# Second attention of a two-layer network: scores of the second half moved in front of both outputs, keys of the second half behind them

## What is computed

```python
x = x + L0_xattn(layernorm(x), ctx)   # 16 heads of 8
x = x + L0_ffn(layernorm(x))          # 8 experts, the best two of each token
x = x + L1_xattn(layernorm(x), ctx)   # 16 heads of 64, low-rank parts, 4 extra context tokens
x = x + L1_ffn(layernorm(x))          # router, 16 experts, each takes 32 tokens of a batch

# L1_xattn, of one batch:
q_in = x @ Wq + lora(x)
k_in, v_in = org_ctx @ Wk + lora, org_ctx @ Wv + lora        # 124 tokens of the context
out = softmax(q k^T / 8) v + softmax(q ipa_k^T / 8) ipa_v    # ipa: the last 4 tokens
return out @ Wo + bo + lora(out)
```

## Time and profile before

| | |
|---|---|
| Times of 3 runs | 515.51, 519.51, 519.55 us, median 519.51 |
| Profiled execution | 518.3 us, of which the span of the instructions is 516.6 |
| PE busy | 494.2 us, 96% of the span |
| PEld busy | 381.7 us, 74% |
| DVE busy | 355.0 us, 69% |
| ACT busy | 291.0 us, 56% |
| POOL busy | 234.5 us, 45% |
| Chain that ended last | PE 85%, DVE 8%, ACT 2%, issue 2% |
| DMA | 14.48 MB, mean 28 GB/s |

### The profile page before, as it was taken

The page is one execution under the profiler, slowest core; times in us unless marked ns, Lnnn a source line. Parts: engine busy times, 40 slices in busy tenths (PEclk is TensorE's granted clock), DMA queues, the critical chain, the costliest instruction groups (busy, mean ns, idle before and its releaser), DMA issues.

```text
span 516.6 us, 13574 instructions
## 1 busy us (share of the span) xinstructions
PE 494.2 (96%) x5113; PEld 381.7 (74%) x5113; DVE 355.0 (69%) x1000; ACT 291.0 (56%) x984; POOL 234.5 (45%) x331
## 2 busy tenths in 40 slices
PE   4799999999999999999999999999999999999996
PEld 3566766656667777877788776788857897799995
DVE  5788989766695687566875756757966688535553
ACT  3366565454576876657776568665674444413332
POOL 5745545035365434665345753333331990090440
PEclk9999999999899999999999999999999999999999
DMA  8910000000001101111000000022202200001001
GB/s 231 198 34 4 3 3 3 3 3 6 4 0 33 34 2 34 34 33 33 3 2 3 3 3 1 1 65 64 63 1 56 70 0 1 1 13 32 1 2 42
DMA packets 21873, 14.48 MB, mean 28 GB/s; under 512 B 5929, under 2 KB 21137, under 8 KB 21809
## 3 DMA queue, kind: packets, MB, share of 16 engines
q1 hardware_dynamic: 20704, 13.31, 9.7%
q10 hardware_dynamic: 1104, 0.30, 0.3%
HBM read 12.30 MB, written 1.05 MB: 26 GB/s over the span
## 4 chain that ended last, share of the span: by engine, by line
PE 85%; DVE 8%; ACT 2%; issue 2%; DMA 1%; ACTq 1%; POOL 1%; DVEq 0%; POOLq 0%
PE bank L1792 9%; PE bank L1551 6%; PE bank L1558 6%; PE bank L1721 6%; PE bank L1538 5%; PE bank L1510 5%; PE bank L1463 5%; PE bank L1530 5%; PE bank L1801 5%; PE bank L1521 5%; PE bank L1374 5%; PE bank L1808 3%; PE bank L1609 3%; PE bank L1359 3%; PE bank L1344 1%
## 5 line engine op out<-in xcount | busy, mean ns | idle before, releaser
L498 POOL TENSOR_TENSOR work<-work,rsum 128x496 f32<-128x496 f32 x64 | 64.1, 1012 | 122.7 <-DVE rsum L789 122.7
L1150 ACT ACTIVATE work<-bank,negmax 128x124 f32<-128x124 f32 x256 | 89.9, 383 | 52.6 <-DVE ipa_s L775 52.5
L533 POOL TENSOR_SCALAR work<-work,slot 128x128 f32<-128x128 f32 x64 | 49.6, 792 | 48.3 <-DVE slot L864 29.4
L1150 ACT ACTIVATION_READ_ACCUMULATOR work<-bank,negmax 128x1 f32 x256 | 58.0, 226 | 0.0
L1792 PE MATMUL bank<-work 128*128 128x256 f32 x224 | 53.4, 382 | 0.0
L1014 DVE SCALAR_TENSOR_TENSOR work<-work,bank 128x256 f32<-128x256 f32 x64 | 26.9, 421 | 33.0 <-ACT work L1302 32.8
L1302 ACT ACTIVATE work<-bank 128x256 f32<-128x256 f32 x64 | 24.5, 383 | 40.6 <-PE bank L1792 29.1
L306 DVE TENSOR_TENSOR x_all<-bank,x_all 128x128 f32<-128x128 f32 x16 | 4.7, 292 | 59.5 <-PE bank L1721 57.1
L481 POOL TENSOR_TENSOR work<-work 128x512 f32<-128x512 f32 (+2 forms) x48 | 39.2, 818 | 12.1 <-DVE work L745 9.6
L1792 PEld LDWEIGHTS bank<-work 128*128 128x128 f32 x224 | 40.4, 191 | 4.6 <-DVE work L1017 0.2
L773 DVE TENSOR_REDUCE negmax<-bank 128x4 f32<-128x496 f32 x64 | 42.5, 664 | 0.0
(11 more groups left out here) (197 smaller groups left out, 1109.7 us busy)
## 6 DMA issues: line engine op xcount, KB each, us to landing
work<-in_L_ffn_w_dram SPq DMA_DIRECT2D x42, 128.0 KB, 2.3
x_all<-in_x_dram SPq DMA_DIRECT2D x4, 256.0 KB, 5.7
out_dram<-x_all SPq DMA_DIRECT2D x4, 256.0 KB, 2.5
ctx_all<-in_ctx_dram SPq DMA_DIRECT2D x4, 192.0 KB, 5.9
ctx_all<-in_L_ffn_w_dram SPq DMA_DIRECT2D x6, 128.0 KB, 2.2
work<-in_L_xattn_Wq_dram SPq DMA_DIRECT2D x1, 512.0 KB, 6.2
work<-in_L_xattn_Wo_dram SPq DMA_DIRECT2D x1, 512.0 KB, 9.0
work<-in_L_ffn_We_dram SPq DMA_DIRECT2D x1, 512.0 KB, 6.5
```

What stands on the lines that cost most here:

```text
L498: pool.tensor_tensor(part, part, rsum1[:, b % 2, CH * n:CH * n + CH].unsqueeze(2).broadcast_to((128, CH, ORG)), ALU.mult).then_inc(Z.norm, 1)
L533: ins = pool.tensor_scalar(ohw_of(e)[:, k, :], count[:, :], slot[:, h, 0, k, e % E1:e % E1 + 1], slot[:, h, 1, k, e % E1:e % E1 + 1], ALU. ...
L1150: ins = act.activation(p1[:, b % 2, n, c, 0:ORG], blocks(bank[n])[:, c, 0:ORG], ACT.Exp, bias=negmax1[:, b % 2, h:h + 1], accum_out=sums1[ ...
```

## The change

It moves calls and changes no computation. On TensorE, `scores(b, 1)` goes from behind ffn 0 to behind ffn 1, directly in front of outputs 0; keys 1 goes behind outputs 1; and ffn 0 goes in front of queries 1, except in the rounds of `head_of`. On ScalarE, `weighted(g)` goes in front of the copy of queries 1 (except in those rounds), the copy of outputs 1 and the extra tokens in front of the copy of keys 1, and powers 2 and 3 behind the copy of inputs. On VectorE, `shifted` 2 and 3 go behind `weighted`, `summed` 1 in front of the copy of turn 2, and `ipa_norm` in front of `summed` 2 and 3. On GpSimd, `experts_sum` goes in front of norms 2 and 3. The core of the diff:

```diff
@@ gpsimd, round1
                     rstds(b + 3, b + 4)
+                if there(b + 4):
+                    experts_sum(b + 4)
                 if there(b):
                     norm(b, 2)
                     norm(b, 3)
-                if there(b + 4):
-                    experts_sum(b + 4)
@@ vector, round1
-                if there(b):
-                    shifted(b, 2)
                 if b == 12:
                     hidden(0)
+                if there(b):
+                    summed(b, 1)
                 if there(t):
                     turned(t, 2)
...
-                if there(b):
-                    shifted(b, 3)
                 if there(f):
                     dve.wait_ge(Z.k0, f + 1)
...
                 if there(g):
                     weighted(g, bank[7])
                 if there(b):
-                    summed(b, 1)
+                    shifted(b, 2)
+                    shifted(b, 3)
                 if b == 15:
                     onehot(3)
                 if there(b):
+                    ipa_norm(b)
                     summed(b, 2)
                     summed(b, 3)
-                    ipa_norm(b)
@@ scalar, round1
                 if there(b):
                     powers(b, 1)
+                if there(g) and not j:
+                    weighted(g, bank[7])
                 if b == 15:
                     turned(t, 1)
                 if there(f):
                     queries(f, 1)
...
-                if there(g):
+                if j:
                     weighted(g, bank[7])
-                if there(b):
-                    powers(b, 2)
...
-                if there(b):
-                    powers(b, 3)
...
-                if there(b):
-                    act.activation(ipa_s[:, b % 2, :, :], ipa_s[:, b % 2, :, :], ACT.Exp).then_inc(Z.ipa_exp, 1)
...
                 if there(t):
                     outputs(t, 0)
+                if b == B:
+                    gathered(6)
+                if there(t):
+                    outputs(t, 1)
+                if there(b):
+                    act.wait_ge(Z.maxed, CH * b + 4)
+                    act.activation(ipa_s[:, b % 2, :, :], ipa_s[:, b % 2, :, :], ACT.Exp).then_inc(Z.ipa_exp, 1)
...
-                if there(t):
-                    outputs(t, 1)
...
                 if there(b + 2):
                     inputs(b + 2)
+                if there(b):
+                    powers(b, 2)
+                    powers(b, 3)
                 if there(f):
                     values(f, 0)
@@ tensor, round1
                 if j:
                     head_logits(j, bank[7])
+                elif there(g):
+                    after(pe, Z.xT, b + 2)
+                    ffn(g, 0, bank[7])
                 if there(f):
                     queries(f, 1, *((Z.p_sb, CH * t + 1) if there(t) else (Z.q_sb, 2 * f)))
...
-                if there(g):
-                    if j:
-                        pe.wait_ge(F.step, HEAD_STEPS * j + 1)
+                if j:
+                    pe.wait_ge(F.step, HEAD_STEPS * j + 1)
                     ffn(g, 0, bank[7])
-                if there(b):
-                    scores(b, 1)
...
                     ffn(g, 1, bank[7])
+                if there(b):
+                    scores(b, 1)
+                if b == 15:
+                    gather(2)
+                    tell(3, G.xg, 2)
                 if there(t):
                     outputs(t, 0, *p_copied(t, 2))
+                if b == B:
+                    gather(6)
+                if there(t):
+                    outputs(t, 1, *p_copied(t, 3))
...
                 if there(f):
                     keys(f, 1, Z.k0_sb, f + 1)
...
-                if there(t):
-                    outputs(t, 1, *p_copied(t, 3))
```

More of the change, by code:

```diff
@@ L1203, in round1 @@
             def round1(b):
-                f, t, g = b + 1, b - 1, b + 4
-                if head_of(b):
-                    head_turned(head_of(b), bank[7])
+                f, t, g, j = b + 1, b - 1, b + 4, head_of(b)
+                if j:
+                    head_turned(j, bank[7])
                 if there(b):
@@ L1222, in round1 @@
                     route_tanh(0)
-                if there(g):
+                if j:
                     weighted(g, bank[7])
-                if there(b):
-                    powers(b, 2)
                 if b == 15:
                     gathered(0)
-                if there(b):
-                    powers(b, 3)
-                if b == 15:
                     turned(t, 3)
@@ L1238, in round1 @@
                     turned(t, 3)
-                if there(b):
-                    act.activation(ipa_s[:, b % 2, :, :], ipa_s[:, b % 2, :, :], ACT.Exp).then_inc(Z.ipa_exp, 1)
-                if head_of(b):
-                    head_powers(head_of(b))
+                if j:
+                    head_powers(j)
                 if there(t):
                     outputs(t, 0)
+                if b == B:
[5 more added lines that the diff above has]
+                    act.activation(ipa_s[:, b % 2, :, :], ipa_s[:, b % 2, :, :], ACT.Exp).then_inc(Z.ipa_exp, 1)
                 if b == 12:
@@ L1250, in round1 @@
                     gathered(2)
-                if b == B:
-                    gathered(6)
                 if b == -1:
@@ L1680, in round1 @@
                     route_turn(1, bank[7])
[L1681 to L1685, removed]
                 if there(f):
```

## The result

The changed kernel takes 543.64 us (median of 6 runs, 542.24 to 546.22) against 519.33 us (6 runs, 515.51 to 519.85). The ratio is 1.0499, with a 95% interval of 1.0461 to 1.0538. It is slower by 24 us, where 15.5 were forecast. The profiled execution of it took 545.58 us, its span is 543.8.

The account below looks back on a forecast made before the run. TensorE, busy for the whole 15.58 us of a steady round, was taken as the bound. Terms of 11.2 + 1.2 - 0.4 - 0.3 + 3.8 = 15.5 on the profiled 518.3 gave 533.8, plus 1.2 made 535.0; range 523 to 545.

Parts of the forecast that it names:

- What bounds the kernel, and the drains: Steady rounds: TensorE always busy; array-shape changes fall from six to three, saving 0.5 a round, 15.08 us on TensorE alone.
- What the second scores covered: Fourth turn: reached at 6.0, but ScalarE's chain to the copy of queries 1 takes 6.99; TensorE stands 1.0, round +0.5.
- Powers 2 and 3 late, xn held: Start of next round: late summed(b, 3) and held xn delay first shifted from 1.20 to 1.92; round 16.82, +1.24.
- the part of the lock: Shared port of VectorE and GpSimd: norm(b, 3) holds xn; a round costs +1.24 with it, +0.86 without.
- The sum: Whole kernel: steady rounds 11.2 and special rounds added to 15.5 us more, giving 535.0.
- The term of the steady rounds: Nine rounds (2 to 4, 6 to 11) at +1.24 each, 11.2 us together.
- alike: Rounds 10 and 11, with more VectorE work on both sides of the change, priced as steady rounds at +1.24 each.
- That stretch: Round 15 to the last projection: +1.8 for round 15 and about +2.0 for the last round, +3.8 together.
- rival (1): TensorE stays the bound and only the drains go: 14 x 0.5 = 7 less, 512.5; chance 0.05.
- Rival (2): TensorE's stand stays near its floor, xn not held, tail covered: 0.5 to 0.86 a round, 522 to 530; chance 0.18.
- Rival (3): Stands of 1.7 in 13 rounds lower the clock in a third to all: +7 to +22, 542 to 557; chance 0.12.
- The range: Time of the changed kernel: 523 to 545 us, likeliest 535, about 0.1 chance below and 0.1 above.

Follow-up runs that it names:

- keys_last: Kernel before, with only keys 1 behind outputs 1 on TensorE and ScalarE's copy of outputs 1 before that of keys 1; 516.18 us, ratio 0.9967.
- mended: Changed kernel: weighted after copy of queries 1, summed 2 and 3 at round's end, second expert half behind outputs, VectorE's weighted behind shifted 3; 514.15 us.
- Experts_first: Kernel before, with only first expert half before queries 1 on TensorE and weighted before the copy of queries 1 on ScalarE; 517.72 us, ratio 0.9996.
- sums_last: Changed kernel, with summed 2 and 3 on VectorE moved from in front of the residual to the end of the round; 525.05 us.
- norm_after_xn: Changed kernel, with GpSimd's norm(b, 3) waiting until VectorE has written xn(b + 3); 536.75 us, ratio 1.0370.
- filled: Changed kernel, with eight unread transposes added on TensorE in front of the fourth turn of rounds 1 to 14; 544.79 us, ratio 1.0511.
- copy_first: Changed kernel, with weighted(g) on ScalarE behind the copy of queries 1 again; 538.82 us, ratio 1.0390.

## Why the prediction was right or wrong, point by point

**What bounds the kernel, and the drains:** right. The block lengths of 0.92 to 0.99 came out, keys_last measured them alone as 0.31 to 0.34 us of the 0.34 worked out, in the rounds without a new wait, and mended has rounds of 15.17 where 15.08 were summed. The Trainium skill's rule that a change of tiling mode drains TensorE (TensorEngine Tiling (Array Packing), Key Properties) holds with these sizes; used alone it would have given the wrong sign for this change.

**What the second scores covered:** right, and shown from both sides. Experts_first has the same ScalarE chain under cover and costs nothing; the changed kernel has it bare and stands 1.39 us. ScalarE's chain took 4.88 us from the first powers to the end of the copy, 4.92 were summed.

**Powers 2 and 3 late, xn held:** right in mechanism, and nearly in size. The first shifted came at 1.80, not 1.92, the turn at 7.69, not 7.74. Sums_last took away the whole of it (0.59 a round), norm_after_xn the part of the lock (0.41). In sums_last the first shifted starts at 1.20 and the copy of queries 1 ends at 6.96, as summed (6.99); the turn comes at 7.10, 0.14 later, as it comes 0.15 behind the copy in the changed kernel, where I had counted 0.03 for the signal.

**The sum:** this is the step that failed. The term of the steady rounds held to 0.01 us. Outside them the profiled span grew by some 10 us more than summed (27.2 without the 1.5 of the first attention, against 15.5). The wrong step is that the special rounds were priced as if VectorE's steps behind summed(b, 3) were those of a steady round: I had counted only onehot(4) as queued there, and had taken rounds 10 and 11 "alike". At the end of round 9 three steps that make masks (`picks`) stand between summed(9, 3) and the residual:

```profile
303.13 0.18 DVE L789 RECIPROCAL rsum<-sums 128x4 f32<-128x4 f32 x1 [1.20 <-ACT work L1149]
303.22 0.34 DVE L804 TENSOR_REDUCE e_mask<-ident 128x16 f32<-128x128 f32 x1
...
304.34 0.28 DVE L306 TENSOR_TENSOR x_all<-bank,x_all 128x128 f32<-128x128 f32 x1
```

These 1.1 us, on top of the late summed, put the first shifted of round 10 at 3.27 of the round instead of 1.65. Its +3.93 are 1.24 as summed, 1.1 for the masks and 1.6 for the clock. In filled and in copy_first, without a drop, round 10 costs 1.1 more than a steady round does; in sums_last, where the masks can run early, 0.2 more. Round 14, forecast +1.1, took +3.3. There the same place holds, at the end of round 13, the probabilities and the first eight of the router. VectorE and TensorE at the start of round 14 of the changed kernel:

```profile
375.64 0.18 DVE L789 RECIPROCAL rsum<-sums 128x4 f32<-128x4 f32 x1 [1.20 <-ACT work L1149]
375.73 0.26 DVE L833 TENSOR_REDUCE ex_sum<-probs 128x1 f32<-128x128 f32 x1
...
378.14 0.29 DVE L306 TENSOR_TENSOR x_all<-bank,x_all 128x128 f32<-128x128 f32 x1
```

```profile
378.49 1.16 PE L1530 MATMUL bank<-xT,work 128*128 128x128 f32 x8 [1.63 <-DVE x_all L306]
```

Before, these 2.4 us of router steps ran while TensorE made the outputs and the projection; now they cannot start before powers(13, 3) are done, and the residual behind them, for which TensorE's queries wait, comes 3 us into the round. At the end of round 14 it is the same with `eight(0, 3)` and `places(0)`. The rule that I had applied to the residual, name what is queued behind the waiting instruction, was not applied round by round. Sums_last, which lets these steps run early, took 2.7 us off round 14, and 5.0 off the stretch behind it. That stretch was forecast +3.8 and took +6.4; 1.2 of the 2.6 between them is the second half of the clock's drop there, as measured above; by my estimate from this price the whole drop cost about 2.4, so here it is the clock, and in rounds 10 and 14 the queue, that the sum had at nothing. In round 12, forecast -0.6, a wait of TensorE that I took as lost (queries 1, for VectorE's copy) grew from 0.32 to 1.03 us instead, and the round took +0.6. Round 13 came as forecast. Rounds 1 and 5 were priced at -0.2 each and cost +0.4 and +0.2, round 0 at -0.3 and cost nothing; why is not shown.

**The rivals:** rival (1), TensorE as the bound, fell; its value is near the one that mended comes to, by other orders (514.15 against its 512.5). Rival (2) fell by the size of the steady rounds. Rival (3), the clock, struck in part, in one of the nine rounds with the long stand and in round 15 of the profiled execution, where it cost 1.6 and about 2.4 us; I had it as an alternative to the forecast, a third of the rounds or more, and it came on top.

**The range** ended at 545; by its ratio on the median that I started from (519.51), the changed kernel stands at 545.4. It was cut too low for the reasons of the sum, nearly all of which point one way.

## What to carry to other kernels

When work is moved out from between two steps of the engine that sets the time, add up what every other engine has to do between the same two points; the work moved was the cover of the longest such chain, and the swap that costs nothing under it costs the difference without it. A step that starts to wait for a late result holds everything behind it in its engine's order, so go through the special rounds one by one, since what stands behind it differs there. A move that is right on one engine may need the others mended: here the second scores in front of the outputs cost 5% and, with four steps placed otherwise (two on VectorE, one on ScalarE, one on TensorE), gained 0.75%.

## What the runs showed of the hardware that I had not expected

Each change of array shape cost TensorE about 0.1 us ahead and 0.05 to 0.1 behind, and a step straight from the 64-row scores to the 64-column outputs costs what the others do (scores to outputs 1.09 us, as scores to a turn). A norm on GpSimd that started 0.37 us before xn on VectorE made a 0.33 us instruction 0.74 us long, and a norm that waits for xn removed this without a change to VectorE. The granted clock fell to its lower level 0.2 us behind an idle time of 1.38 us (at 312.0 us), though the eight other stands of that length left it alone, and in round 15 it fell 1.6 us into an idle time of 2.48 us; I have no explanation that these runs bear out.
